# Second attention: one transposed piece for both heads' last 64 keys, half-length value products on it, second head's keys in reversed groups

## The reference, cut to what matters

```
for start in range(0, L, 128):                 # a block of 128 queries
    ks = max(0, start - 64)                    # 64 keys before the block, and its own 128
    s = jnp.einsum('bhqd,bhkd->bhqk', q[:, :, start:end], k[:, :, ks:end]) * scale
    s = jnp.where(qi >= ki, s, -jnp.inf)       # a query sees no later key
    a = jax.nn.softmax(s, axis=-1)
    outs.append(jnp.einsum('bhqk,bhkd->bhqd', a, v[:, :, ks:end]))
```

## Time and profile before

| | |
|---|---|
| median of three runs | 3144.66 us |
| the profiled execution's own time (its span) | 3149.4 us |
| second attention in it, about | 1626 to 3149 us |
| TensorE busy, matmuls | 3012.4 us (96%) |
| VectorE, ScalarE, GpSimd busy | 2118.6, 1863.2, 1017.1 us |
| median distance of two local strides | 10.85 us |

### The profile page before, as it was taken

One profiled execution on the slowest core, in us unless ns is written; L12 is line 12 of the kernel. 1 busy time (PEld: TensorE's weight loads), 2 busy tenths in 40 slices (PEclk: granted clock), 3 DMA queues, 4 the chain that ended last, 5 costly groups with the idle time before them and its releaser, 6 DMA issues. The chain is left out here.

```text
span 3149.4 us, 66407 instructions
## 1 busy us (share of the span) xinstructions
PE 3012.4 (96%) x23638; PEld 2264.0 (72%) x23638; DVE 2118.6 (67%) x5888; ACT 1863.2 (59%) x4638; POOL 1017.1 (32%) x1627
## 2 busy tenths in 40 slices
PE   7999999999999999997988999999999999999998
PEld 5888888853444444434877888788887888788886
DVE  5666666678989989975655555655556555555556
ACT  4666666647877778773445555455554555455553
POOL 0000000001100000001016666576656666566663
PEclk9999999989999999998999999999999999999999
DMA  4111111232333232103224444344443444244432
GB/s 150 50 48 48 48 48 41 60 68 44 69 50 64 35 75 45 30 9 116 83 69 110 99 101 94 103 122 101 94 107 93 114 103 95 67 114 105 102 87 68
DMA packets 296707, 246.35 MB, mean 78 GB/s; under 512 B 149180, under 2 KB 231740, under 8 KB 296252
## 3 DMA queue, kind: packets, MB, share of 16 engines
q1 hardware_dynamic: 296380, 242.11, 31.7%
HBM read 100.71 MB, written 44.04 MB: 46 GB/s over the span
## 5 line engine op out<-in xcount | busy, mean ns | idle before, releaser
L1838 ACT ACTIVATE b_pp<-b_pp,b_nm 128x192 f32<-128x192 f32 (+2 forms) x1024 | 472.8, 463 | 447.6 <-DVE b_nm L2005 366.1
L1007 ACT ACTIVATE a_pt<-ps 128x512 f32<-128x512 f32 x1024 | 556.1, 595 | 178.9 <-PE ps L1043 177.9
L176 DVE TENSOR_REDUCE mx<-ps 128x2 f32<-128x1024 f32 x512 | 622.3, 1224 | 58.6 <-PE ps L167 44.0
L1808 POOL TENSOR_SCALAR b_pp<-b_pp,b_rc 128x192 f32<-128x192 f32 x960 | 389.2, 428 | 383.9 <-DVE b_rc L2014 383.9
L2026 DVE COPY b_pt<-ps 128x384 f32<-128x384 f32 (+2 forms) x336 | 182.1, 556 | 316.7 <-PE ps L1927 301.4
L2005 DVE CUSTOM_DVE_ANT_0 b_pp<-ps,b_mk 128x192 f32<-128x192 f32 x960 | 276.3, 354 | 136.8 <-PE ps L1906 136.8
L797 DVE SCALAR_TENSOR_TENSOR f_yac<-ps,f_cw,f_yac 128x128 f32<-128x128 f32 x992 | 278.1, 344 | 125.3 <-PE ps L596 123.0
L596 PEld LDWEIGHTS ps<-w,f_sq 128*128 128x128 f32 x2048 | 265.2, 191 | 26.5 <-issue 6.0
L596 PE MATMUL ps<-w,f_sq 128*128 128x128 f32 x2048 | 270.2, 275 | 0.3
L1961 PE MATMUL ps<-b_wo,b_oT 128*128 128x256 f32 x1024 | 241.6, 380 | 3.7 <-ACT b_vv L1831 3.7
L1056 PE MATMUL ps<-a_pt,a_v 128*32 128x256 f32 x3072 | 242.0, 395 | 0.0
(11 more groups left out here) (282 smaller groups left out, 7332.8 us busy)
## 6 DMA issues: line engine op xcount, KB each, us to landing
b_rt<-b_qf SPq DMA_DIRECT2D x1024, 64.0 KB, 2.0
qk_parts<-f_aa SPq DMA_DIRECT2D x32, 512.0 KB, 2.7
v_rows<-f_va_ SPq DMA_DIRECT2D x16, 512.0 KB, 2.8
rl<-in_W1qT SPq DMA_DIRECT2D x64, 128.0 KB, 2.6
rl<-in_W1kT SPq DMA_DIRECT2D x64, 128.0 KB, 2.7
rl<-in_W1vT SPq DMA_DIRECT2D x32, 256.0 KB, 3.2
b_wo<-in_W1oT SPq DMA_DIRECT2D x16, 512.0 KB, 4.2
b_vs<-b_vv SPq DMA_DIRECT2D x60, 128.0 KB, 2.9
```

The costliest lines, as they stand in the source:

```text
L176: e.tensor_reduce(M["mx"][kh % 3][:, :, jt, h], P.pair(s), AX.X, ALU.max, negate=True).then_inc(P.free_sem(s), 1)
L1007: e.activation(pt[(4 * i + 2 * j + a) % 12][:, :], P.ap((*s, a)), ACT.Exp).then_inc(P.free_sem((*s, a)), 1)
L1808: m = e.tensor_scalar(x, x, r[:, 2 * u + h:2 * u + h + 1], 1.0, ALU.mult, ALU.mult)
L1838: e.activation(x, x, ACT.Exp, bias=nm[n % 4][:, c:c + 1], scale=-1.0, accum_out=sm[n % 4][:, c:c + 1]).then_inc(exp_done, 1)
```

## The change

- The second head's 192 keys are put into the scores in reversed groups of 64 (last 64, first 64 of the block, 64 before it). In `first` its moving operand becomes a three-group access pattern with a negative step. The mask for it, `turned`, is a new tile with the same groups.
- The three transposed pieces become: the first head's keys 0 to 127; both heads' last 64 keys; the second head's other 128 keys. The piece of the last keys is transposed first, into columns 192 to 319 of the bank, and the third piece then overwrites columns 192 to 255, the queries for which the last keys' weights are zero. 320 columns are copied to `pt`, where it was 384.
- In `fourth` the two products with the shared piece stream 64 columns (queries 64 to 127) into the block's last 64 output columns, where they streamed 128.
- `vs` gets the second head's values (128 columns per block, was 64), and `vb` holds the last 64 keys' values. `earlier` issues six DMAs, was four.
- Four more DMAs and two memsets at the start of the phase fill `turned`; the waits count up to the new numbers. The scratch area for software DMA is made smaller (1024), which frees the room for the larger tiles.

```
@@ sync @@
             e.dma_start(mk0[:, 64:192], A["mask"]).then_inc(mask_in, 16)
+            for i in range(2):
+                for j in range(2):
+                    e.dma_start(turned[:, i, 64 * j:64 * j + 64],
+                                A["mask"][:, 64 - 64 * j:128 - 64 * j]).then_inc(mask_in, 16)
@@ sync, earlier @@
-                    e.dma_start(vs[x][0:64, 1:NQ, :], v[64:128, 0:NQ - 1, at:at + 64]).then_inc(vb_in[x], 16)
-                    e.dma_start(vs[x][64:128, :, :], v[0:64, :, at:at + 64]).then_inc(vb_in[x], 16)
+                    e.dma_start(vs[x][0:64, 1:NQ, 0:64], v[64:128, 0:NQ - 1, at:at + 64]).then_inc(vb_in[x], 16)
+                    e.dma_start(vs[x][64:128, :, 0:64], v[0:64, :, at:at + 64]).then_inc(vb_in[x], 16)
+                    e.dma_start(vs[x][0:64, :, 64:128], v[0:64, :, at + 64:at + 128]).then_inc(vb_in[x], 16)
+                    e.dma_start(vs[x][64:128, 1:NQ, 64:128], v[64:128, 0:NQ - 1, at + 64:at + 128]).then_inc(vb_in[x], 16)
                     e.dma_start(vb[x][0:64, :, 0:64], v[64:128, :, at:at + 64]).then_inc(vb_in[x], 16)
-                    e.dma_start(vb[x][64:128, 1:NQ, 64:128], v[64:128, 0:NQ - 1, at + 64:at + 128]).then_inc(vb_in[x], 16)
+                    e.dma_start(vb[x][64:128, :, 64:128], v[64:128, :, at + 64:at + 128]).then_inc(vb_in[x], 16)
@@ tensor, first @@
-                                m = e.matmul(scores(u, h), q[r, d:d + 128], kk[r, d:d + 192], start=True, stop=True)
+                                keys = kk[r, d:d + 192]
+                                if h:
+                                    keys = keys.rearrange("p (c k) -> p c k", c=3)[:, ::-1, :]
+                                m = e.matmul(scores(u, h), q[r, d:d + 128], keys, start=True, stop=True)
@@ tensor, third @@
-                        for c in range(3):
-                            at = 384 * s[2] + 128 * c
-                            m = e.transpose(P.ap(f)[:, c * 128:(c + 1) * 128], pp[n % 3][:, at:at + 128], ident[:, :])
-                        m.then_inc(P.full_sem(f), 1)
+                        y, at = P.ap(f), 384 * s[2]
+                        e.transpose(y[:, 192:320], pp[n % 3][:, at + 128:at + 256], ident[:, :])
+                        e.transpose(y[:, 0:128], pp[n % 3][:, at:at + 128], ident[:, :])
+                        e.transpose(y[:, 128:256], pp[n % 3][:, at + 256:at + 384],
+                                    ident[:, :]).then_inc(P.full_sem(f), 1)
@@ tensor, fourth @@
-                            e.matmul(o0, vs[x][:, i + u, :], y[:, 0, :], start=u == 0, stop=False)
-                            e.matmul(o1, v[:, i + u, right + 64:right + 128], y[:, 2, :], start=u == 0, stop=False)
-                            e.matmul(o0, vb[x][:, i + u, 0:64], y[:, 1, :], start=False, stop=u == 3)
-                            e.matmul(o1, vb[x][:, i + u, 64:128], y[:, 1, :], start=False, stop=u == 3).then_inc(pv_done, 1)
+                            l0, l1 = o0[:, 64:128], o1[:, 64:128]
+                            e.matmul(o0, vs[x][:, i + u, 0:64], y[:, 0, :], start=u == 0, stop=False)
+                            e.matmul(o1, vs[x][:, i + u, 64:128], y[:, 1, :], start=u == 0, stop=False)
+                            e.matmul(l0, vb[x][:, i + u, 0:64], y[:, 2, 0:64], start=False, stop=u == 3)
+                            e.matmul(l1, vb[x][:, i + u, 64:128], y[:, 2, 0:64], start=False, stop=u == 3).then_inc(pv_done, 1)
...
```

More of the change, by code:

```diff
@@ L1620, in second_attention @@
         bob = sb("bob", [128, 256])
-        mk, mk0 = sb("mk", [128, L]), sb("mk0", [128, 192])
+        mk, mk0, turned = sb("mk", [128, L]), sb("mk0", [128, 192]), sb("turned", [128, 2, 192])
         xh = [M["xh"], sb("xh1", [128, 2, L], FR)]
@@ L1630, in second_attention @@
         vb = [sb(f"vb{i}", [128, NQ, 128]) for i in range(2)]
-        vs = [sb(f"vs{i}", [128, NQ, 64]) for i in range(2)]
+        vs = [sb(f"vs{i}", [128, NQ, 128]) for i in range(2)]
         pp = [sb(f"pp{i}", [128, 2 * L]) for i in range(3)]
@@ L1845, in scalar @@
                         w.wait_ge(pv_done, x - 4)
-                        e.activation(pt[x % 5][:, 0:3, :].rearrange("p a b -> p (a b)"), P.ap(f)[:, 0:384],
+                        e.activation(pt[x % 5][:, :, :].rearrange("p a b -> p (a b)")[:, 0:320], P.ap(f)[:, 0:320],
                                      ACT.Copy).then_inc(P.free_sem(f), 1)
@@ L1889, in tensor @@
                     half, at = i // 4, P.at[s][0]
-                    w.wait_ge(set_up, 4)
+                    w.wait_ge(set_up, 6)
                     for x in range(2):
@@ L1946, in tensor @@
                         x = vb_of(t) % 2
-                        w.wait_ge(vb_in[x], 64 * (vb_of(t) // 2 + 1))
+                        w.wait_ge(vb_in[x], 96 * (vb_of(t) // 2 + 1))
                         for u in range(4):
@@ L1968, in vector @@
             e.memset(mk0[:, :], -3e38).then_inc(set_up, 1)
+            e.memset(turned[:, 0, 128:192], 0.0).then_inc(set_up, 1)
+            e.memset(turned[:, 1, 128:192], -3e38).then_inc(set_up, 1)
             for z in kp:
@@ L1986, in vector @@
                     at = P.at[s][0]
-                    w.wait_ge(mask_in, 48)
+                    w.wait_ge(mask_in, 112)
                     w.wait_ge(*P.filled(s))
@@ L2003, in vector @@
                             for h in range(2):
-                                mask = mk[:, L - 192:L] if i + u else mk0[:, :]
+                                if h:
+                                    mask = turned[:, 0 if i + u else 1, :]
+                                else:
+                                    mask = mk[:, L - 192:L] if i + u else mk0[:, :]
                                 m = e.tensor_tensor_reduce(
@@ L2021, in vector @@
                         else:
-                            lo, hi = 0, 384
+                            lo, hi = 0, 320
                         if whole(t) or not on_act(i + s[2]):
@@ L2175 @@
     from concourse.bass_utils import run_bass_kernel_spmd
-    nc = bacc.Bacc("TRN2", target_bir_lowering=False, num_devices=1)
+    nc = bacc.Bacc("TRN2", target_bir_lowering=False, num_devices=1, dynamic_dma_scratch_size=1024)
     arrays, A = {}, {}
```

## The result

Over 20 runs each, the changed kernel takes **3151.11 us** (3138.32 to 3171.97), the kernel before 3143.23 us (3136.77 to 3149.07). The ratio is 1.0028, 95% interval 1.0016 to 1.004. The forecast was 3133 us, faster; the change made the kernel slower by 7.9 us. The range, 3099 to 3166, holds the time.

The account below looks back on a forecast made before the run. TensorE's own work was taken to bound the second attention, with ScalarE's wait for key weights close to binding. From the profiled 3149.4: -49 + 35 + 2 = 3137.4, written as 3133 us after allowing for that run's offset; range 3099 to 3166.

Parts of the forecast that it names:

- Short value products, -49: TensorE's value products in local strides: short pairs take 0.058 us instead of 0.109, -49 us (bounds -53 and 0).
- no cheaper: Rival on the value products: a short pair stays at 0.109 us, 3171 us; chance 0.16, in part or wholly.
- Reversed keys, 0: Scores with the second head's keys in reversed groups stream as plain operands do: 0, at most +1.57 us a stride.
- Transposes, copies and the fourth reading, 0: Reordered transposes, smaller PSUM copies, and TensorE's load waiting for the fourth reading of the scores: 0 each.
- Start of the phase, +2: Four mask DMAs ahead of the first weights delay ScalarE's copies that free banks for TensorE: +2 us (0 to +2).
- Two more DMAs, +35: SyncE's queue in local turns: weights 1.37 us later, so ScalarE's key-weight waits become TensorE stalls, +35 us.
- the foretold signs: In the changed profile: ScalarE's key-weight wait over 120 us in all, TensorE's idle time ahead of the scores about 45 us.
- the allowance of 2.18 us: How late ScalarE's key-weight step may start before TensorE's scores are late; put at 2.18, between 2.15 and 2.20 readings omitted.
- 1.78 us: Growth of each ScalarE key-weight wait: ScalarE and TensorE 0.41 us earlier in the stride, weights 1.37 later.
- 0.40: A wait of w becomes a stall of w - 0.40; waits shorter than that put some 2.5 us back.
- +24 and +68: Other sizes of the weight-delay loss: loads only 1.0 us late, +24; one DMA more each turn taking 1.60, +68.
- The jam as a rival: SyncE's queue: one DMA more per turn is held up, +21, 3166 us; chance 0.13.

Follow-up runs that it names:

- kernel 1: The changed kernel with SyncE issuing the query, key and value weight loads ahead of the six DMAs of `earlier`: 3088.71 us, ratio 0.9829.
- kernel 2: The kernel before with only the reordering, weight loads ahead of the four DMAs of `earlier`: 3133.28 us, ratio 0.9974.
- kernel 4: Kernel 1 with all four value products of a block streaming 128 columns again (output changed): 3135.02 us, ratio 0.9982.
- kernel 7: Kernel 1 with the second head's keys in plain order, no negative step (output changed): 3088.32 us, ratio 0.9822.
- kernel 6: Kernel 1 with the four turned-mask DMAs issued behind the value weights of the first turns: 3083.28 us, ratio 0.9812.
- kernel 3: The kernel before with six DMAs in `earlier`, two of them filling a half of `vs` that nobody reads; products unchanged: 3171.32 us, ratio 1.0095.
- kernel 9: The changed kernel, SyncE's queue untouched, with ScalarE's step that waits for the key weights one slot later: 3090.68 us, ratio 0.9842.
- kernel 5: Kernel 3 with the two added DMAs cut to one of the 8 blocks of a head: 3165.51 us, ratio 1.0065.

## Why the prediction was wrong, step by step

- **Short value products, -49: right.** The rows have pairs 0.055 to 0.056 us apart (0.058 assumed) and undisturbed strides of 10.42 to 10.43 (10.44 foretold): 120 x 0.425 = 51. Kernels 1 and 2 give -44.6, kernel 4 gives -46.3. The rival "no cheaper" is out. The Trainium skill (TensorE: Matmul & The Clock Gate, Wait — 56ns, not 53.3ns?) has about 62 ns for each matmul with hardware decode off; here a block's two short instructions, four records in all, take 0.11 us, which is 28 ns a record and 56 ns an instruction, so by neither reading does that figure bind here. By it the gain would be gone (per record) or 960 x (0.109 - 0.062) = 45 us (per instruction; an estimate); the second is too near for the totals to tell, and the rows decide.
- **Reversed keys, 0: right** (kernel 7). **Transposes, copies and the fourth reading, 0: right**; nothing of them became a wait of the scores.
- **Start of the phase, +2: small**, between 0 and 5 (kernel 6).
- **Two more DMAs, +35: this is the step that failed.** Its mechanism is right to the line: kernel 3 shows it alone, kernels 1 and 9 remove it at either end, and the foretold signs came (wait of ScalarE over 120 us: 161.8; TensorE idle at the scores about 45 us: 52.2). The size is too small: TensorE's stall grew by 40.6 us, not 35, and the clock came on top (next point). What was wrong in the 35 is the allowance of 2.18 us, read from one stride and taken for all. Of the 30 stalls after, 26 lie 1.94 to 2.27 us below the wait of ScalarE that belongs to them. The other four are the first of the phase, at 1646.67, 1676.48, 1699.93 and 1720.98 us, and lie only 0.18 to 0.53 below: 3.52 less 3.00 in the rows above. In a later stride 1.73 us of output projection (L1973) stand between the last transposes and the scores, as the chain has it at 2235.33; the first output projection of the phase starts at 1740.7. Until then TensorE is ready for the scores 1.73 us sooner, which leaves 2.18 - 1.73 = 0.45. In these four turns waits of 19.3 us became stalls of 18.0, where 2.18 gives 10.5. Over all waits after, 2.18 everywhere gives 45.4 us, and 0.45 for these four gives 52.3; measured are 52.2. The kernel before shows it too, and the earlier trace rows had it: the longest wait, 7.7, became a stall of 7.2.

```profile
1675.61 0.63 ACT L1819 ACTIVATE w1b_h<-rl 128x512 fp32r<-128x512 f32 x1 [7.67 <-DMA rl<-in_W1kT]
1676.87 2.93 PE L1906 MATMUL ps<-b_kp,b_qp 64*128 64x192 f32 x16 [7.19 <-ACT b_vv L1831]
```

- **Where the waits grew.** The prediction added 1.78 us to each of the 37 waits that existed; they grew by 1.63 on average. The queue is longer in all 59 turns that load key weights, so 22 new waits came, of 1.91 on average. They explain why the 161.8 lies so far above the "over 120", but not the stall: most lie within the allowance, and they stalled TensorE for 1.7 us in all. Of the 37 old waits six are shorter than 0.40, which puts 0.7 us back, not 2.5.
- **The clock, without a term.** From 1610 us on, the profile of the kernel before has 17.6 us at 1.2 GHz, that of after 44.9; kernels 1 and 3 have 15.9 and 19.6. 27.3 us more at half clock cost at most 13.7 us, since the same work would take half the time at full clock. A single profile can mislead here. The record has the mean granted clock of every run, over the whole program; from its medians the time at half clock is some 69 us before (41 runs beside the experiments), 94 after, 68 in kernel 1, and 82 in kernels 3 and 5. Within the 20 runs of the changed kernel the time goes with it (correlation -0.93 with the mean clock), some 0.37 us for each us at half clock, and within the 41 runs of the kernel before, some 0.30 (-0.92). For 25 us more that is 8 to 9 us (an estimate). So the term of +35 was really 40.6 + 8 to 14, or 49 to 55. The runs say the same without any row: the late weights cost the changed kernel 62 us (over kernel 1) and the kernel before 8 to 9 (over kernel 2), that is 53 to 54 more.

The sum with the measured terms: -51 + 40.6 + 8 to 14 + 0 to 5 = -2 to +9 us; measured +7.9. Three short waits of the scores for L1997, 2.9 us in all, vanished behind the longer ones and would take that much off. Two sums close to each other in size were subtracted, so an error of 20 us in one turned the sign: the forecast of -12 stood on a gain that came within some 3 us, and on a loss bounded only by +24 and +68. The loss measured lies a little above the middle of these bounds, and the middle (46) would have said "within 0.2%".

The jam as a rival (one DMA more per turn is held, +21) is not what happened: of the issues of `earlier`, 34 of 360 took over 0.95 us, where 18 of 240 did before; one more in each of 60 turns would have been 60 more. Its price, though, was nearer to the truth than the forecast.

**Open.** Why single issues are held for about 1 us is not known; no kernel took them away. The clock's share is known only to some 6 us, and why the clock fell after five of the seven stalls of over 2 us and not after the other two, one of them the longest, the runs don't tell. The share does go with the kernels: kernel 3 lost 28.7 us, of which 22.9 are stalls, and by the medians of its runs it has 13 us more at half clock, worth 4 to 5 at the rates above. Its one profile (19.6 against 17.6) doesn't show this.

## What to carry to other kernels

Before adding a DMA to a queue, look at what stands behind it in the same turn and who waits for that: here two issues of 0.7 us each, on an engine that computes nothing, took back the whole gain of a shorter TensorE stream, and putting the urgent loads ahead of them gave it back (3151 to 3089 us). Where an engine waits for a transfer, move that instruction behind the copies that others need, or the load ahead; one of the two is enough. An allowance read from one stride holds for strides of that kind: look for those that lack a part of the work, and check it against the longest wait of the list. And when a forecast is a difference of two terms of like size, its sign is no surer than the worse known of them.

## What the runs showed of the hardware that was not expected

- A stall can cost more than its length: after 2.3 to 2.9 us of idle time TensorE was granted 0.50 of its clock for 3.4 us (1834.6 and 2097.4, after), and the scores took 2.14 and 2.93 us instead of 1.57. It need not: after 3.00 us (1699.93, after) and 2.62 us (1658.46, kernel 3) the clock stayed full. At 2097.4 TensorE was busy for most of the slow stretch:

```profile
2094.00:2097.40 3.40, 1.16 (x6) 0.68 (x4) 0.65 (x3) 1.20 (x3) 1.62 (x3) 1.00 0.60 155
2097.40:2100.80 3.40, 3.33 (x20) 2.93 (x22) 0.36 (x3) 0.03 (x1) 3.40 (x9) 0.50 0.50 121
```

- Most of these DMAs take a slot of 0.60 to 0.70 us on SyncE's queue, whether they move 64 pieces or some 500 (kernels 3 and 5), and about one in twenty (78 of the 1653 from 1626 us on, after) is held for over 0.95 us.
- A moving operand of three groups in reversed order cost nothing that these runs can tell: 323 ns a record either way (kernel 7).
